# A new order of the loop step on TensorE, ScalarE and VectorE of a 32-batch attention and feed-forward kernel

## What is computed

```python
def _L0_attn_ref(x, ln_w, ln_b, wq, wk, wv, wo):      # x: 32 x 256 x 128, 16 heads of 8
    y = _layernorm(x, ln_w, ln_b)
    q, k, v = (einsum('bsd,hde->bhse', y, w) for w in (wq, wk, wv))
    scores = einsum('bhse,bhte->bhst', q, k) / sqrt(HEAD) + causal
    attn = einsum('bhst,bhte->bshe', softmax(scores), v)
    return attn.reshape(...) @ wo + x
x = _layernorm(x + _L0_attn_ref(x, ...))
x = _layernorm(x + (x @ (W + up_aux @ lora_up @ lora_down @ down_aux).T + b))
```

## Time and profile before

| | |
|---|---|
| median of 3 runs | 437.22 us |
| the profiled execution, its own time | 438.39 us |
| its span, first to last instruction | 436.7 us |
| mean granted TensorE clock | 0.989 |
| busy: PE, DVE, ACT, POOL | 418.1, 381.4, 342.1, 308.0 us |
| one loop step | 12.2 us |

### The profile page before, as it was taken

How to read it: one execution, slowest core, us unless ns; L and a number is a source line. 1 busy time by engine, 2 the same in 40 slices (tenths; PEclk the granted TensorE clock), 3 DMA queues, 4 the chain that set the end, 5 groups by cost and what they waited for, 6 DMA issues and landing times.

```text
span 436.7 us, 15760 instructions
## 1 busy us (share of the span) xinstructions
PE 418.1 (96%) x5571; PEld 335.9 (77%) x5571; DVE 381.4 (87%) x1056; ACT 342.1 (78%) x865; POOL 308.0 (71%) x395
## 2 busy tenths in 40 slices
PE   7698999999999999999999999999999999998994
PEld 3366677888888888888888888888888888877762
DVE  4589978999999999999999999999999999988664
ACT  2376777788888888888888888888888888887871
POOL 6764857777777777777777778777777777754763
PEclk9699999999999999999999999999999999999998
DMA  2566576665775667666676666666676676555111
GB/s 77 151 171 170 152 190 148 164 169 155 196 192 164 180 173 175 179 174 165 176 194 176 171 166 178 173 173 169 161 193 183 170 176 175 147 140 137 42 49 38
DMA packets 77915, 69.16 MB, mean 158 GB/s; under 512 B 9307, under 2 KB 68530, under 8 KB 77874
## 3 DMA queue, kind: packets, MB, share of 16 engines
q1 hardware_dynamic: 76446, 67.68, 59.2%
q10 hardware_dynamic: 1428, 0.95, 0.9%
HBM read 47.07 MB, written 21.00 MB: 156 GB/s over the span
## 4 chain that ended last, share of the span: by engine, by line
PE 84%; DVE 5%; DMA 4%; SPq 2%; ACT 2%; issue 2%; POOL 0%; POOLq 0%; ACTq 0%; DVEq 0%
PE pv_bank L1363 20%; PE score_bank L1344 12%; PE bank L1376 11%; PE bank L1371 8%; PE max_bank L1330 7%; PE max_bank L1326 6%; PE max_bank L1331 6%; PE score_bank L1345 6%; PE bank L1433 3%; PE bank L1434 3%; DVE rowmax L1042 2%; DMA kx<-k_rows 2%; PE score_bank L1420 1%; DMA q_rows<-parts 1%; ACT qx L670 1%
## 5 line engine op out<-in xcount | busy, mean ns | idle before, releaser
L1042 DVE TENSOR_REDUCE rowmax<-max_bank 128x2 f32<-128x512 f32 (+1 forms) x384 | 245.8, 675 | 16.5 <-PE max_bank L1331 8.8
L615 ACT ACTIVATE probs<-score_bank 128x384 f32<-128x384 f32 x512 | 222.3, 491 | 39.1 <-PE score_bank L1345 26.5
L512 POOL TENSOR_SCALAR_AFFINE_SELECT probs<-probs 128x1024 f32<-128x1024 f32 x127 | 137.8, 1095 | 56.6 <-ACT probs L615 56.4
L1344 PE MATMUL score_bank<-qx,kx 74*128 74x256 bf16 x512 | 119.9, 273 | 0.5 <-DMA qx<-mT 0.5
L1345 PE MATMUL score_bank<-qx,kx 74*128 74x128 bf16 x512 | 101.6, 218 | 0.0
L1363 PE MATMUL pv_bank<-probs,v_ext 128*32 128x256 f32 x2032 | 97.5, 329 | 0.0
L1330 PE MATMUL max_bank<-kx,qx 128*128 128x128 bf16 x512 | 86.6, 221 | 2.3 <-DVE rowmax L1042 2.3
L1331 PE MATMUL max_bank<-kx,qx 74*128 74x128 bf16 x512 | 86.2, 220 | 0.0
L1363 PEld LDWEIGHTS pv_bank<-probs,v_ext 128*32 128x32 f32 x2032 | 56.3, 109 | 31.9 <-issue 6.8
L1330 PEld LDWEIGHTS max_bank<-kx,qx 128*128 128x128 bf16 x512 | 48.6, 98 | 15.0 <-issue 5.9
L1344 PEld LDWEIGHTS score_bank<-qx,kx 74*128 74x128 bf16 x512 | 49.7, 97 | 6.5 <-issue 1.6
(11 more groups left out here) (123 smaller groups left out, 615.7 us busy)
## 6 DMA issues: line engine op xcount, KB each, us to landing
kx<-k_rows SPq DMA_DIRECT2D x187, 96.0 KB
qx<-q_rows SPq DMA_DIRECT2D x128, 96.0 KB
qx<-q_rows SPq DMA_DIRECT2D x64, 104.0 KB
q_rows<-parts SPq DMA_DIRECT2D x32, 192.0 KB, 2.2
k_rows<-parts SPq DMA_DIRECT2D x31, 192.0 KB, 2.4
xa<-in_x SPq DMA_DIRECT2D x32, 128.0 KB, 3.9
xr<-in_x SPq DMA_DIRECT2D x32, 128.0 KB, 2.3
out<-y SPq DMA_DIRECT2D x32, 128.0 KB, 3.4
```

The source lines that it names most:

```text
L512: pool.affine_select(out=t, in_=t, compare_op=ALU.is_ge, fill=0.0, base=0, pattern=[[0, GROUP * NB], [1, P]], channel_multiplier=-1)\
L615: act.activation(probs[:, h, 0:PW], score_bank[SCORE_BANK[h]][:, 0:PW], ACT.Exp, scale=SCALE / Q_SCALE)\
L1042: dve.tensor_reduce(to, of, AX.X, ALU.max).then_inc(s_mread[unit], 1)
L1344: pe.matmul(b[:, 0:SEQ], k[0:SCORE_ROWS, i, 0:P], q[0:SCORE_ROWS, i, :], start=True, stop=True)
```

## The change

It is in the order of things alone; no operation is added or taken away. Four kinds of edits:

1. `scores` gets an argument `wide_last`: the product of 128 columns first, that of 256 last. In `step` it is set for heads 9, 10, 12 to 15 and 0, 2, 4, 5, 6, 8. `max_scores` makes the two products of depth 128 first and then the two of depth 74, everywhere.
2. In most helpers of ScalarE, VectorE, GpSimd and in `pv` the wait for what comes late is now the last of the waits.
3. `step` on TensorE, ScalarE and (one pair) VectorE is written in another order. On VectorE `divide(it, 0, 0)` comes before `row_max(it, 2, 10)` instead of behind it.
4. `first` and `last` keep their order.

```diff
 def scores(it, o, h, wide_last=False):
...
+    if wide_last:
+        pe.matmul(b[:, SEQ:PW], k[0:SCORE_ROWS, i, P:SEQ], q[0:SCORE_ROWS, i, P:SEQ], start=True, stop=True)
+        pe.matmul(b[:, 0:SEQ], k[0:SCORE_ROWS, i, 0:P], q[0:SCORE_ROWS, i, :],
+                  start=True, stop=True).then_inc(s_score[h], 1)
...
 def max_scores(it, o, unit):
...
+    h = quad * GROUP + 2 * (kind - 1)
     for g in range(2):
-        h = quad * GROUP + 2 * (kind - 1) + g
-        pe.matmul(b[:, g * SEQ:g * SEQ + P], q[:, h, P:SEQ], k[:, h, P:SEQ], start=True, stop=True)
-        ins = pe.matmul(b[:, g * SEQ + P:g * SEQ + SEQ], q[0:SCORE_ROWS, h, P:SEQ],
-                        k[0:SCORE_ROWS, h, 0:P], start=True, stop=True)
+        pe.matmul(b[:, g * SEQ:g * SEQ + P], q[:, h + g, P:SEQ], k[:, h + g, P:SEQ], start=True, stop=True)
+    for g in range(2):
+        ins = pe.matmul(b[:, g * SEQ + P:g * SEQ + SEQ], q[0:SCORE_ROWS, h + g, P:SEQ],
+                        k[0:SCORE_ROWS, h + g, 0:P], start=True, stop=True)
...
 def first_parts(it, o):
-    act.wait_ge(s_qk, it.done(o))
     act.wait_ge(s_q_stored, it.done(o - 1, 16))
     act.wait_ge(s_stored, it.done(o - 1, STORES))
+    act.wait_ge(s_qk, it.done(o))
...
 def residual(it, o):
+    dve.wait_ge(s_xr, it.done(o, 16))
+    if it.static:
+        dve.wait_ge(s_zT, it.done(o - 1))
     dve.wait_ge(s_wo, it.done(o))
-    dve.wait_ge(s_xr, it.done(o, 16))
-    if it.static:
-        dve.wait_ge(s_zT, it.done(o - 1))
```

```diff
 # ScalarE, step: the end
                 if it.runs(4):
                     first_parts(it, 4)
-                if it.runs(1):
-                    exp(it, 1, 8)
-                if it.runs(4):
                     second_parts(it, 4)
                 if it.runs(0):
                     copy_pv(it, 0, 1)
                 if it.runs(4):
                     copy_v(it, 4)
+                if it.runs(-3):
+                    normalize_f(it, -3)
+                if it.runs(1):
+                    exp(it, 1, 8)
+                    exp(it, 1, 9)
                 if it.runs(2):
                     copy_maxT(it, 2)
-                if it.runs(1):
-                    exp(it, 1, 9)
-                if it.runs(-3):
-                    normalize_f(it, -3)
```

More of the change, by code:

```diff
@@ L808, in step @@
                     exp(it, 0, 13)
-                    copy_pv(it, 0, 0)
                     exp(it, 0, 14)
                     exp(it, 0, 15)
-                if it.runs(1):
-                    exp(it, 1, 0)
+                    copy_pv(it, 0, 0)
                 if it.runs(-1):
@@ L822, in step @@
                 if it.runs(1):
-                    exp(it, 1, 4)
-                    exp(it, 1, 5)
+                    exp(it, 1, 2)
+                    exp(it, 1, 3)
                 if it.runs(-1):
@@ L827, in step @@
                 if it.runs(1):
+                    exp(it, 1, 4)
+                    exp(it, 1, 5)
                     exp(it, 1, 6)
@@ L1086, in residual, with scale_ff @@
                                          op0=ALU.mult, op1=ALU.add).then_inc(s_z, 1)
-            def scale_ff(it, o, bank=bank7, made=()):
-                dve.wait_ge(s_ff, it.done(o))
-                dve.wait_ge(*(made or (s_rs, turns(it, o - Z_AT))))
+            def scale_ff(it, o, bank=bank7, made=(), scale_last=False):
                 if it.static:
                     dve.wait_ge(s_y, it.done(o - 2))
+                scaled, multiplied = made or (s_rs, turns(it, o - Z_AT)), (s_ff, it.done(o))
+                for signal, count in (multiplied, scaled) if scale_last else (scaled, multiplied):
+                    dve.wait_ge(signal, count)
                 if not it.static:
@@ L1226, in step @@
                 if it.runs(2):
+                    row_max(it, 2, 10)
                     row_max(it, 2, 11)
@@ L1633, in step @@
                     values(it, 3)
-                if it.runs(0):
-                    scores(it, 0, 9)
-                    scores(it, 0, 10)
+                if it.runs(-1):
+                    pv(it, -1, 2)
+                    pv(it, -1, 3)
+                if it.runs(2):
+                    max_scores(it, 2, 0)
                 if it.runs(1):
@@ L1670, in step @@
                 if it.runs(0):
-                    scores(it, 0, 14)
+                    scores(it, 0, 14, wide_last=True)
                 if it.runs(2):
@@ L1703, in step @@
                 if it.runs(1):
-                    scores(it, 1, 4)
-                    scores(it, 1, 5)
+                    scores(it, 1, 3)
                 if it.runs(2):
@@ L1720, in step @@
                         pe.wait_ge(s_yT, it.done(4))
+                        pe.wait_ge(s_z, it.done(-1))
                     z_transpose(it, -1)
+                if it.runs(0):
+                    if it.static:
+                        bank_free(it, (s_z, -1), (s_aTs, -1), (s_f, -2), (s_norm[1], -1), (s_vx, 3), (s_norm[0], -1))
+                    pv_transpose(it, 0, 0)
+                if it.runs(1):
+                    scores(it, 1, 5, wide_last=True)
                 if it.runs(2):
@@ L1735, in step @@
                 if it.runs(2):
+                    max_scores(it, 2, 10)
+                if it.runs(1):
+                    scores(it, 1, 7)
+                if it.runs(2):
                     max_scores(it, 2, 11)
+                if it.runs(1):
+                    scores(it, 1, 8, wide_last=True)
             def last(at):
```

111 lines of the change are left out of this document (49 added, 62 removed).

## The result

| | before | after |
|---|---|---|
| median of 4 runs | 438.23 us (436.68 to 439.35) | 447.15 us (443.48 to 449.22) |
| ratio after / before | | 1.018, 95% interval 1.014 to 1.023 |
| profiled execution, span | 438.39, 436.7 us | 445.28, 443.6 us |
| from the start to pv of group 2 in step 2, the first `step` | 66.4 us | 66.7 us |
| the 26 steps from there | 318.0 us | 323.4 us |

The forecast was 436.3 us, range 432.0 to 441.5. The last three lines are read from the starts of the pv products; they say where the 6.9 us of span went: 5.4 in the steps, 1.1 at the end, 0.3 at the start. (The 438.23 us of before have one run more than the 437.22 us that the forecast started from.)

What follows compares the result with a forecast made beforehand. The prediction took TensorE, 96% busy, to bound the kernel. 26 step lengths x -0.08 us = -2.1, with +1.2 at the kernel's end, gave -0.9 off the median of 437.22: 436.3 us, range 432.0 to 441.5.

## What to carry to other kernels

When an edit delays what stands at the head of an in-order queue, list every consumer behind it, and compare each room with the slowest case in the trace, not the usual one; spare time that shows as no wait at all may be hiding a tail of 2 us. Count what a consumer needs from the first issue to the last landing. And price waits, too: their order was worth 0.7% here.

## What the runs showed of the hardware

- SyncE's issues, 0.36 us each, took 0.7 to 1.8 us eleven times in 125 us while code ran for the first time, and none did so in some 200 us of loop behind.
- A transfer of 8 KB that landed over 2.5 us behind its issue had an instruction packet start meanwhile in 77 of 97 cases, one that landed sooner in 76 of 715.
- An operation that carries the late wait behind separate instructions for early ones started 0.06 (ScalarE) to 0.10 us (VectorE) later than one whose late wait was a separate instruction ahead.
- A change of depth between neighbouring products costs 4 ns each (59 instead of 55 ns from start to start).
